# VectorE compares the chunk numbers of ten columns in two instructions of five columns each, in both edge sorts of a graph network

## What is computed

```python
h = jnp.maximum(_layernorm(x, axis=-1), 0.0)
x = x + _L0_gnn_ref(h, edge_weight, edge_index)      # two segment sums: over src and over dst
h = jnp.maximum(_layernorm(x, axis=-1), 0.0)
x = x + _L1_gnn_ref(h, W_heads, ..., edge_index)     # attention, two segment sums over src

# inside _L0_gnn_ref
row, col = (edge_index[0], edge_index[1])
x_fwd = segment_sum(w * x[col, :c_half], row, num_segments=n) / clip(deg_row, 1.0)[:, None]
x_bwd = segment_sum(w * x[row, c_half:], col, num_segments=n) / clip(deg_col, 1.0)[:, None]
```

## Time and profile before

| what | us |
|---|---|
| median of 3 runs | 3130.86 |
| time of the profiled execution | 3138.38 |
| its span in the trace | 3136.6 |
| VectorE busy | 2162.2 (69%) |
| TensorE busy | 2368.6 (76%) |
| GpSimd busy | 2049.6 (65%) |
| ScalarE busy | 1589.7 (51%) |

### The profile page before, as it was taken

One profiled execution on the slowest core, in us unless ns is written; L12 is line 12 of the kernel. 1 busy time (PEld: TensorE's weight loads), 2 busy tenths in 40 slices (PEclk: granted clock), 3 DMA queues, 4 the chain that ended last, 5 costly groups with the idle time before them and its releaser, 6 DMA issues. The chain is left out here.

```text
span 3136.6 us, 48973 instructions
## 1 busy us (share of the span) xinstructions
PE 2368.6 (76%) x16450; PEld 1814.2 (58%) x16450; DVE 2162.2 (69%) x4446; ACT 1589.7 (51%) x4526; POOL 2049.6 (65%) x2003
## 2 busy tenths in 40 slices
PE   1777689888898789875667788888884677777761
PEld 1677688878888688853334444444443555555551
DVE  9999888878887698843226588888877433434337
ACT  0454466656665566643333445545547555555544
POOL 1010277777777777777774577777766477777772
PEclk7999899989999799975558899999996887887775
DMA  2001011111112411122226577777780233333352
GB/s 63 1 1 43 16 46 45 45 47 47 46 47 46 49 45 45 44 58 51 51 52 82 175 209 209 210 208 210 208 181 8 74 107 105 106 106 106 106 96 57
DMA packets 114891, 270.64 MB, mean 86 GB/s; under 512 B 34543, under 2 KB 51670, under 8 KB 114646
## 3 DMA queue, kind: packets, MB, share of 16 engines
q0 software_dynamic: 89088, 245.53, 31.4%
q1 hardware_dynamic: 25558, 21.98, 2.1%
HBM read 250.96 MB, written 16.42 MB: 85 GB/s over the span
## 5 line engine op out<-in xcount | busy, mean ns | idle before, releaser
L388 POOL DMA_INDIRECT rows_near<-table_a,s_idx_S x464 | 534.8, 1153 | 227.5 <-issue 112.5
L1039 DVE TENSOR_TENSOR work<-work,bank 128x129 f32 (+2 forms) x928 | 390.4, 421 | 302.9 <-PE bank L725 208.7
L388 POOL DMA_INDIRECT rows_near<-table_b,s_idx_D x464 | 500.0, 1078 | 141.4 <-issue 105.4
L388 POOL DMA_INDIRECT rows_near<-table,s_idx_S x464 | 446.7, 963 | 173.6 <-issue 124.3
L388 POOL DMA_INDIRECT given<-table,s_idx_S x464 | 448.0, 965 | 141.3 <-issue 124.6
L725 PE MATMUL bank<-rows_near,oh 128*128 128x129 f32 x1856 | 385.3, 341 | 180.8 <-ACT rows_near L497 146.9
L711 PE MATMUL bank<-scratch 128*128 128x224 bf16 (+1 forms) x2520 | 401.7, 270 | 110.2 <-DVE scratch L1014 77.4
L841 PE MATMUL bank<-scratch,oh 128*128 128x512 f32 x928 | 448.7, 629 | 21.3 <-DVE scratch L1197 21.3
L711 PE MATMUL bank<-rows_near,sort_ring 128*128 128x224 bf16 (+1 forms) x2520 | 403.0, 271 | 68.4 <-ACT sort_ring L488 39.8
L725 PEld LDWEIGHTS bank<-rows_near,oh 128*128 128x128 f32 x1856 | 295.2, 227 | 258.4 <-ACT rows_near L497 189.8
L580 ACT ACTIVATE e_att<-lrelu 128x32 f32<-128x32 f32 (+1 forms) x232 | 50.4, 217 | 606.0 <-DVE lrelu L1186 606.0
(11 more groups left out here) (198 smaller groups left out, 4431.3 us busy)
## 6 DMA issues: line engine op xcount, KB each, us to landing
rows_near<-table_a,s_idx_S POOLq DMA_INDIRECT x464, 2.7
rows_near<-table_b,s_idx_D POOLq DMA_INDIRECT x464, 2.7
rows_near<-table,s_idx_S POOLq DMA_INDIRECT x464, 3.6
given<-table,s_idx_S POOLq DMA_INDIRECT x464, 3.6
table<-scratch SPq DMA_DIRECT2D x25, 260.0 KB, 2.1
table<-scratch SPq DMA_DIRECT2D x25, 128.5 KB, 2.9
xs<-in_x SPq DMA_DIRECT2D x1, 3072.0 KB
out_x<-scratch SPq DMA_DIRECT2D x24, 128.0 KB, 1.7
```

Of the source, the lines that this page charges most:

```text
L388: nc.gpsimd.indirect_dma_start(out=to, out_offset=None, in_=table[:, :], in_offset=bass.IndirectOffsetOnAxis(ap=s_idx[order][:, c:c + 1], ...
L1039: v.tensor_add(a, a, psum).then_inc(sum_free[o], 1)
```

## The change

The comparison of L1009 is written as a loop of two instructions. Each covers five of the ten columns. Buffers, values, waits and everything that follows stay as they were. It is in `place_batch`, so it holds for all four parts.

```diff
                 v.tensor_tensor(two(oh_lane[slot]), across(iota_lane[:, :], P), along(lane[o], P), ALU.is_equal).then_inc(lane_ready, 1)
-                v.tensor_tensor(two(oh_chunk[slot][:, :, 0:width]), across(iota_chunk[:, CUT[h]:CUT[h + 1]], width),
-                                along(chunk[o], width), ALU.is_equal)
+                for j in range(0, BATCH, BATCH // 2):
+                    there = slice(j, j + BATCH // 2)
+                    v.tensor_tensor(two(oh_chunk[slot][:, there, 0:width]), across(iota_chunk[:, CUT[h]:CUT[h + 1]], width)[:, there],
+                                    along(chunk[o], width)[:, there], ALU.is_equal)
                 dve.wait_ge(lane_ready, n + 1)
```

## The result

The changed kernel takes 3078.54 us (median of 4 runs, 3076.74 to 3081.97) where the kernel before takes 3130.47 us (median of 4): a ratio of 0.9832, 95% interval 0.9818 to 0.9845, or 51.9 us less. The forecast was 3065 us. The profiled execution after is 3078.84 us, so between the two profiled executions, 3138.38 and 3078.84, lie 59.5 us; the sum of the prediction was made between these and said 66.3.

A forecast was written before the change was run, and what follows sets the result against it. VectorE was taken to bound part 0, GpSimd's rate of gathers parts 1 to 3. From 3138.38 us, -23.2 - 23.2 - 22.8 + 2.9 = -66.3 us, carried to the median: 3065 us (3055 to 3085 at 0.64; range 3042 to 3105).

The forecast's parts named there:

- the sum of the prediction: Whole kernel: parts 1 to 3 win 23.2, 23.2 and 22.8 us, part 0 loses 2.9; together -66.3 us.
- The bound: Parts 1 to 3 are bound by GpSimd's rate of gathers (323.4 of 325 us in part 1), part 0 by VectorE.
- The rule for a gather's length, and its release between the halves: A gather starting in a VectorE instruction with two SBUF inputs ends 0.90 us after that instruction; otherwise it takes 0.94.
- The walk: Gather starts followed through steady batch steps of parts 1 to 3: nine gathers in two steps, 4.5 a step against 4.
- The slower rival: No release between the halves, four gathers a step stay: +11.8 us, 3143 us (3156 with 0.15 us fixed); chance 0.09.
- The fixed part of an instruction: Each of 168 batches pays 0.07 us for the added VectorE instruction; +2.9 us in part 0, step 6.24 to 6.31.
- The sum for a part: 42 steps x 0.5 = 21 gathers at 1.24 us, -26.1 us, less 2.9 for longer steps: -23.2 us.
- capped by VectorE's waits: Part 3 can win no more than VectorE's `col_free` waits, 25.7 us, less 2.9: 22.8 us.
- From the profiled execution to the median: Profiled 3138.38 us less 66.3 gives 3072.1; being 7.5 us above the median, carried to it: 3064.6, forecast 3065.
- the stages shifted and nothing else: Sign expected in the changed kernel's profile: the attention stages after 1700 us are only shifted.

The follow-up runs named there:

- one and nine: The kernel before with the comparison cut into one and nine columns: 3144.64 us beside 3137.74 us for the kernel before, ratio 1.0023.
- eight and two: The kernel before with the comparison cut into eight and two columns: 3148.28 us beside 3136.44, ratio 1.0039; on the TensorE-paced chip ratio 0.9989.
- the input in PSUM: The kernel before with the list of chunk numbers for parts 1 to 3 in PSUM, not SBUF: 3165.34 us beside 3129.15.
- The swap: The kernel before and the changed kernel, both with the halves cut at 240 chunks and not 224: 3128.58 and 3076.69 us.

## Why the prediction came out as it did

- **The bound.** Right. GpSimd issued gathers without a gap over 0.3 us in both traces, and what its gathers lost in waits came off the time: 61.3 us less busy, 59.5 us less in all, with part 0's cost between (see the last item).
- **The rule for a gather's length, and its release between the halves.** Right, and now shown by experiment: by the cut (one and nine, eight and two) and by the input in PSUM. That L1008 and L1031 hold gathers too, which was assumed, is so: after the change 58 of the 62 gathers that start in L1008 take over 0.96 us, and 100 of the 117 in L1033.
- **The walk.** Right to 0.01 us in the steady steps, nine gathers in two of them. The slower rival, no release between the halves, is refuted.
- **The fixed part of an instruction.** 0.07 us was forecast. Part 0 from its first L1008 to its last takes 277.9 us against 274.7 before, so 3.2/42 = 0.076 us, and 3.2 us against 2.9. The batch step went from 6.24 to 6.31. That the first gather starts 4.1 us later, and not 3.2, has nothing to do with the change: the first L1008 starts at 77.77 us against 76.96, and both values occur in other runs, with and without a split in part 0.
- **The sum for a part.** Mis-sized. Forecast: -23.2, -23.2 and -22.8 us. Measured from a part's first step to the first one behind its 52 steps: 306.4 to 286.3, 303.1 to 290.3 and 295.7 to 274.1 us, so -20.1, -12.8 and -21.6. Part 3 was capped by VectorE's waits, as I had it: 2.6 us of them are left. By the gathers' busy time beside each part it is -20.1, -14.8 and -23.1 us, so the term that failed is above all part 2's 42 x 0.5 gathers. It took every batch step for a steady one. But in part 2 eight batch steps began with a long wait, and in these the gathers lost 0.77 us on average in place of the 1.18 of a steady step, so there was less to win; and in the changed kernel 13.2 and 15.8 us of waits are left in parts 1 and 2, not 11 and 9. The swap shows that the chunk width has a hand in it, for 3 to 4 us; the rest stays open. The whole of the walk's gain was to be 69.2 us in the three parts, and the gathers' busy time fell by 61.3 in the whole of layer 0, of which 58.0 lie beside the parts.
- **From the profiled execution to the median.** The forecast took the difference between two profiled executions and laid it at the median of before. That execution lay 7.9 us above the median (3138.38 against 3130.47), and after's lay at it (3078.84 against 3078.54). Of the 14.4 us between forecast and measured gain (66.3 and 51.9), 7.6 us lie here and 6.8 in the terms. The 6.8 are a balance: the gathers gave 8.0 us less than the 69.2, the first gather starts 4.1 us later and not 2.9, and 2.4 us came off behind the last gather, where the prediction had the stages shifted and nothing else; that last one is luck. I had named the 7.5 us of the profiled execution and had no reason for them; none of the runs shows one.

## What to carry to other kernels

When one engine issues gathers without a pause, look at how long each gather's instruction takes and at what the other engine runs when it starts: a long instruction can cost the issuer its whole length, and cutting it may be worth far more than the instruction added. Walk through one period of the two engines before choosing the cut, since the outcome comes in whole gathers for a period: five and five won 1.7%, eight and two lost 0.4%, with the same count of instructions. And check that issuing is the bound: on the chip where TensorE set the pace, the same edit shortened the gathers and won nothing. A late start of the next engine on the gathered rows doesn't say that they landed late; look at what that engine waited for first.

## What the runs showed of the hardware

- An indirect DMA of 128 rows whose row numbers lie in SBUF is held while VectorE runs an instruction with two SBUF inputs: it ends 0.90 us after the start of VectorE's next instruction, which is 0.81 us after the end that the profile gives for the one it waited for (515.64 beside 514.75 and 514.83 in the trace of before). It needs this only at its start. One that starts 0.04 us earlier takes 0.94 us, and VectorE's instruction beside it isn't longer for it (0.82 us).
- With one of the two inputs in PSUM, the same comparison holds nothing, but it takes 2.65 us and not 1.40 for 2400 elements (that input being fp32 there).
- One more VectorE instruction in an unbroken row cost 0.076 us.
- The same kernel took 3130 us on one chip and 3496 us on another, and there TensorE bounded the gather stages, with 199 us of gaps without a releaser from 368 to 1630 us and a granted clock of 0.819 against 0.858. The gathered rows landed as soon after the gather on both.
